# Graph attention layer: the values' matmuls moved from the end of each group of four units to its middle

## The reference

```python
feats   = einsum('bnf,hfo->bhno', h, kernel)
f_self  = einsum('bnf,hfd->hbnd', h, attention_kernel)
f_other = einsum('bnf,hfd->hbdn', h, attention_kernel_2)
scores  = einsum('hbnd,hbdm->hbnm', f_self, f_other)
masked  = a * scores
masked  = where(masked >= 0, masked, 0.2 * masked) / sqrt(16)
masked  = masked + where(a == 0, -1e9, 0)
attn    = softmax(masked, axis=-1) * where(a == 0, 0, 1)
out     = relu(einsum('bhnm,bhmo->bhno', attn, feats) + bias)   # heads side by side: 64 columns
return layernorm(x + out, axis=-1)
```

## Time and profile before

| | |
|---|---|
| median of 3 runs | 928.04 us (927.79 to 928.58) |
| the profiled execution, its own time | 928.04 us |
| its span in the profile | 926.2 us |
| PE busy | 868.7 us (94%) |
| DVE busy | 785.4 us (85%) |
| ACT busy | 630.3 us (68%) |
| POOL busy | 299.8 us (32%) |
| mean granted TensorE clock | 0.973 of full speed |

### The profile page before, as it was taken

One profiled execution on the slowest core, in us unless ns is written; L12 is line 12 of the kernel. 1 busy time (PEld: TensorE's weight loads), 2 busy tenths in 40 slices (PEclk: granted clock), 3 DMA queues, 4 the chain that ended last, 5 costly groups with the idle time before them and its releaser, 6 DMA issues.

```text
span 926.2 us, 14045 instructions
## 1 busy us (share of the span) xinstructions
PE 868.7 (94%) x4956; PEld 279.7 (30%) x4956; DVE 785.4 (85%) x1509; ACT 630.3 (68%) x1244; POOL 299.8 (32%) x280
## 2 busy tenths in 40 slices
PE   4089999999999999999999999999999999999994
PEld 3022332233233233333322332332333333222231
DVE  3168889988999989898899889999899988999994
ACT  2057776777677776777767776777767777677773
POOL 5042081233543063330921335430633309202101
PEclk7579999999999999999999999999999999999998
DMA  9795479853895849926797538947599258974000
GB/s 240 128 259 135 154 122 239 204 154 81 123 277 145 197 86 185 294 59 156 121 258 203 124 107 133 299 117 198 85 202 278 62 153 127 255 182 64 18 1 17
DMA packets 198396, 144.53 MB, mean 156 GB/s; under 512 B 177104, under 2 KB 177104, under 8 KB 198320
## 3 DMA queue, kind: packets, MB, share of 16 engines
q1 hardware_dynamic: 195152, 139.91, 64.5%
q10 hardware_dynamic: 3168, 3.67, 2.4%
HBM read 94.08 MB, written 12.51 MB: 115 GB/s over the span
## 4 chain that ended last, share of the span: by engine, by line
PE 88%; issue 4%; DVE 2%; DMA 2%; SPq 2%; POOL 1%; ACT 0%; POOLq 0%; DVEq 0%
PE z L495 54%; PE numer L519 29%; PE misc L428 2%; DVE z L785 1%; PE misc L470 1%; SPq L220 1%; DMA edges<-in_adj 1%; PE misc L434 1%; DMA x_sb<-in_x 1%; POOL mask L323 1%; PE misc L421 1%; DVE norm L721 0%; DMA maskT<-mask 0%; DVE ob L807 0%; SPq L212 0%
## 5 line engine op out<-in xcount | busy, mean ns | idle before, releaser
L785 DVE SCALAR_TENSOR_TENSOR z<-z,maskT 128x512 f32<-128x512 f32 (+1 forms) x1152 | 725.4, 680 | 111.7 <-PE z L495 105.0
L690 ACT ACTIVATE probs<-z 128x512 f32<-128x512 f32 (+1 forms) x1152 | 596.9, 593 | 257.9 <-PE z L495 257.9
L495 PE MATMUL z<-self_st,other_st 96*128 96x512 bf16 (+3 forms) x2304 | 561.2, 378 | 25.0 <-issue 24.7
L495 PEld LDWEIGHTS z<-self_st,other_st 96*128 96x128 bf16 (+1 forms) x2304 | 189.6, 98 | 477.0 <-ACT probs L690 306.7
L519 PE MATMUL numer<-probs,vals 128*32 128x512 f32 (+1 forms) x2304 | 301.1, 595 | 0.2 <-ACT probs L690 0.2
L323 POOL TENSOR_SCALAR mask<-edges 128x1500 int16<-128x1500 f32 x96 | 138.3, 1441 | 93.2 <-DMA maskT<-mask 44.7
L368 POOL TENSOR_TENSOR cent<-yb,mean 128x256 f32<-128x256 f32 x24 | 14.7, 612 | 299.0 <-DVE mean L820 299.0
L352 POOL TENSOR_SCALAR part<-proj 128x512 bf16<-128x512 f32 x21 | 12.5, 618 | 218.7 <-ACT proj L625 218.7
L519 PEld LDWEIGHTS numer<-probs,vals 128*32 128x32 f32 x2304 | 45.3, 108 | 118.2 <-ACT probs L690 95.6
L359 POOL TENSOR_TENSOR part<-rest,part 128x512 bf16<-128x512 f32 x21 | 23.7, 1157 | 0.0
L354 POOL TENSOR_TENSOR rest<-proj,part 128x512 f32<-128x512 f32 x21 | 23.7, 1157 | 0.0
(11 more groups left out here) (67 smaller groups left out, 210.0 us busy)
## 6 DMA issues: line engine op xcount, KB each, us to landing
edges<-in_adj SPq DMA_DIRECT2D x88, 750.0 KB, 6.0
parts_dram<-part SPq DMA_DIRECT2D x21, 384.0 KB, 5.6
self_st<-parts_dram SPq DMA_DIRECT2D x42, 192.0 KB, 5.9
other_st<-parts_dram SPq DMA_DIRECT2D x42, 192.0 KB, 6.3
edges<-in_adj SPq DMA_DIRECT2D x8, 468.8 KB
x_sb<-in_x SPq DMA_DIRECT2D x8, 352.0 KB
out<-cent SPq DMA_DIRECT2D x8, 352.0 KB
maskT<-mask SPq DMA_TRANSPOSE x96, 6.4
```

The source lines that it names most:

```text
L495: return nc.tensor.matmul(z[:, v % BUFS * STEP + i, 0:WIDTH[st]], other_st[par][rows, h, c * P:(c + 1) * P], self_st[par][rows, h, st * W: ...
L690: nc.scalar.activation(probs[:, g % PROBS, v % UNITS * STEP:(v % UNITS + 1) * STEP, 0:WIDTH[st]], z[:, v % BUFS * STEP:(v % BUFS + 1) * ST ...
L785: nc.vector.scalar_tensor_tensor(banks, banks, FLOOR, maskT[(par + st) % 2][:, c, 0:WIDTH[st]].unsqueeze(1).broadcast_to([P, STEP, WIDTH[s ...
```

## The change

In the table of PE's order the values of a group move from behind the fourth unit to between the second and the third. Nothing else is changed: no instruction is added or removed, no lag, no semaphore count, and the orders of DVE, ACT, POOL and SP are the same.

```diff
-ORDER = (("s", 0), ("l", 0), ("s", 1), ("l", 1), ("s", 2), ("l", 2), ("s", 3), ("l", 3), ("v", 0))
+ORDER = (("s", 0), ("l", 0), ("s", 1), ("l", 1), ("v", 0), ("s", 2), ("l", 2), ("s", 3), ("l", 3))
```

## The result

The changed kernel takes 950.08 us (median of 4 runs, 949.65 to 951.08) against 928.31 us before (927.79 to 929.0), a ratio of 1.0236 with a 95% interval from 1.0218 to 1.0253. It is slower, as forecast, but by 21.8 us instead of 13.7, and outside the stated range. Run once more, it gave a ratio of 1.0203 (1.0187 to 1.0220). The profiled execution took 949.65 us with a span of 947.9 us, 21.7 us more than that of before.

What follows compares the result with a forecast made beforehand. The prediction took PE as the bound, almost never standing still. It added 9.4 (copy), 4.1 (rounds at units 120 and 124) and 0.2 (ends), 13.7 us, to 928.0 for 941.7 us, range 936.5 to 946.5.

Steps and rivals of the forecast that it cites:

- What bounds the kernel: Steady stretch, 100 to 800 us: PE is the bound and waits only 3.6 us, so the change can gain little.
- The turned pattern costs nothing: Plain groups: moving the values by half a group turns the pattern, and both short windows keep their size; cost nothing.
- Term 1: First values of every stage but the first: they wait for ACT's copy of numer, 23 x 0.41 = 9.4 us.
- The sentence on the Trainium skill: ACT's pace at 512 columns: the page estimates 0.52 us, making the copy's cost 11.0 us; the row's 0.487 decides.
- Term 2: Units 120 and 124: PE waits 1.09 us instead of 0.50 for DVE's reduction, +0.59 us seven times, 4.1 us.
- squares 1.46: Entry in PE's list of times: squares of unit 120 at 1.46 us, counted from the previous group's values' end.
- Term 3: Program's last group: the last unit's lift follows its score by three matmuls, its mask not done; about 0.2 us once.
- Nothing changes up to there: First batch, up to PE's wait for the DMA of x until 78.02: same work ahead as before, no change.
- (a): Batch starts: the flag's load and branch lose their cover, up to 1.1 us at 7 starts, 949.4 us; chance 0.07.
- (b): Stage's first values: the copy of numer is hidden after all, leaving 932.3 us; chance 0.04.
- (c): First score behind the values: gets up to 0.10 us cheaper in 286 groups, 913.1 us; chance 0.03.
- (d): Whole kernel: DVE really sets the pace in the finishing stretches, so no change to the time, 928; chance 0.02.

Runs made afterwards that it cites:

- the kernel with the fitted constants: The changed kernel with the copy of numer behind unit 3, the squares at unit 122 and the transpose at 128: 929.77 us, ratio 1.0001.
- both rounds late in both orders: Squares at unit 128, transpose at 134: in the kernel before 923.99 us; in the changed kernel, with the copy behind unit 3, 928.1 us.
- The second trial: The changed kernel run again unaltered, with more rounds: 949.13 us, ratio 1.0203 to the kernel before.

## Why the prediction was wrong

**What bounds the kernel: right.** PE's pace did not change (1.85 and 0.99 us), no gain was there to be had, and every microsecond of wait was lost.

**The turned pattern costs nothing: right for the plain groups**, whose pace is unchanged at 2.84 us; the two short windows hold. The whole of the new place is not free: the kernel with the fitted constants has a ratio of 1.0001 to the kernel before, but with both rounds late in both orders the middle is 4.1 us slower.

**Term 1, the copy: right mechanism, one part too small.** Count (23), ACT's times (within 0.01 us) and place were as forecast. The part that was mis-sized is PE's answer to the release, taken as 0.05 us from a load in the program's last round; here it was 0.14, since the values have two waits and the one met last is written second. 0.50 to 0.51 a time instead of 0.41, 11.6 us instead of 9.4. The exchange of the two waits took just that part away.

**The sentence on the Trainium skill.** By its page "ScalarE: Activation LUTs", section "What ACT_TABLE_LOAD costs", ACT's pace was to be an estimated 0.52 us and the term 11.0 us. That is near the measured 11.6, but for the wrong reason: the trace has the exponentials 0.49 us apart (501.16 to 501.65), as the row had it, and the copy's end at 2.15.

**Term 2, the rounds at 120 and 124: incomplete.** The wait at L451 came out at 1.07 us against 1.09. What failed is the step "squares 1.46" in the list of PE's times: it took the squares as free to start and never asked what their own wait, `misc_free`, hangs on. It hangs on the finishing step behind unit 118, in the very list that the prediction wrote down for DVE (step at 0.92, so done at 1.25), while the squares were due at 1.13. In the trace the step is done at 1.34 (588.30), and the squares are 0.3 us late in each batch. The sentence "there the last lift was 0.2 us late before, and about as much now" was too low by 0.16. In all 1.02 us a batch instead of 0.59, 7.1 us instead of 4.1.

**Term 3: right**, 0.2 us at the last lift (0.19 in the profile of PE). "Nothing changes up to there" for the first batch was too sure: up to the first load of x nothing in the program asks for more time, but that load's moment lay between 77.28 and 79.97 us in the thirteen profiles, with or without a clock that falls behind it, and the range had no room for it. So of the 8.1 us between forecast and result, 5.5 are the terms (2.2 the copy, 3.0 the rounds, the rest the batch starts) and the rest is mostly chance: 2.0 us are the later x of the profile.

**The rivals.** (a), the branch: its condition was put wrongly, since in the kernel before the read starts while PE is still at work (482.57, with the values behind it), and in the changed kernel nearly nothing shows (2.22 us for ten matmuls, as their widths ask for). But the margin is small, as the kernels with the rounds moved show, where it costs 0.3 to 0.7 us a batch. (b), (c) and (d) were not seen: the wait for the copy is there, the first score behind the values takes 0.32 us as before, and the loss is beyond doubt.

The range was closed at 946.5 by leaving out a corner of its own bounds, which reached 947.8. The second trial lies at 949.1.

## What to carry to other kernels

When one engine's instructions move, list for every instruction in the stretch what releases it, the waits that were always met included: one list of times for each engine, and every semaphore checked against both. A wait's price is the distance between the releasing and the waiting instruction, so constants that tie side work to fixed units have to be moved with the order (ratio 1.0236 without, 1.0001 with). And a wait that is seen at one instruction may be an engine's lack of time over a whole stretch; moving the instruction by a little only moves the wait, moving it out of the stretch removes it (0.9992 against 0.9937).

## What the runs showed of the hardware

- A PE instruction behind two waits answered 0.14 us after the release when the wait met last was written second, and 0.04 when it was written first. The wait written second is a sequencer instruction of its own, 51 ns long.
- After a wait of 1.6 to 2.1 us PE's granted clock fell in six of seven executions (0.72 to 0.91 from 80 to 86 us), after one of 0.8 to 1.0 us in none of six.
- Reading one value into PE's sequencer (L552) took 0.30 to 0.82 us (medians of a run 0.30 to 0.58); what makes the difference was not found. At the batch starts the first weight load behind the branch came 0.82 to 0.99 us after the end of the read, in the kernel before, in the changed one and in the experiments alike.
